# Attention scores from two fp32 parts in 64-row TensorE tiles in place of three bf16 parts in 32-column tiles, with the P.V products regrouped

## The reference, cut to what matters

```python
x = x + attention(layernorm(x))      # 16 heads of 8, softmax over all 512 keys
x = x + moe(layernorm(x))            # shared FFN 128-512-128, plus top 2 of 8 experts
# attention: q, k, v = x W.T + b ; softmax(q k.T / sqrt(8)) v ; out Wo.T + bo
```

## Time and profile before

| | us |
|---|---|
| median of 3 runs | 621.56 |
| span of the profiled execution | 600.2 |
| what lies around the span, by the median | 21.4 |
| PE busy | 585.2 (98%) |
| DVE busy | 497.1 (83%) |
| ACT busy | 452.8 (75%) |
| POOL busy | 280.1 (47%) |

### The profile page before, as it was taken

The page is one execution under the profiler, slowest core; times in us unless marked ns, Lnnn a source line. Parts: engine busy times, 40 slices in busy tenths (PEclk is TensorE's granted clock), DMA queues, the critical chain, the costliest instruction groups (busy, mean ns, idle before and its releaser), DMA issues.

```text
span 600.2 us, 21750 instructions
## 1 busy us (share of the span) xinstructions
PE 585.2 (98%) x8258; PEld 405.9 (68%) x8258; DVE 497.1 (83%) x1076; ACT 452.8 (75%) x967; POOL 280.1 (47%) x481
## 2 busy tenths in 40 slices
PE   6898999999999999999999999999999999999997
PEld 3443556555665655655655765656899999999966
DVE  8989999999999999999999999735577777777557
ACT  5887898888888888888888888985266555555551
POOL 7947430222542542542642642656745555555500
PEclk9999999999999999999999999999999999999999
DMA  6896333324434322322322311001422222222173
GB/s 177 224 303 208 110 80 93 102 79 121 126 91 128 90 57 61 85 57 64 82 57 66 82 56 47 21 20 49 93 56 67 70 70 70 71 70 70 42 294 136
DMA packets 43839, 57.66 MB, mean 96 GB/s; under 512 B 11130, under 2 KB 31482, under 8 KB 43754
## 3 DMA queue, kind: packets, MB, share of 16 engines
q1 hardware_dynamic: 39434, 47.59, 28.1%
q0 software_dynamic: 4320, 8.89, 4.6%
HBM read 35.76 MB, written 20.42 MB: 94 GB/s over the span
## 4 chain that ended last, share of the span: by engine, by line
PE 91%; ACT 3%; SPq 2%; DMA 1%; DVE 1%; issue 1%; POOL 0%; DVEq 0%; ACTq 0%
PE ps L1423 18%; PE ps L1451 18%; PE ps L1466 18%; PE ps L1677 11%; PE ps L1665 11%; PE ps L1624 4%; PE ps L1615 4%; PE ps L1405 2%; PE ps L1655 1%; PE ps L1486 1%; ACT xn L761 1%; PE ps L1411 1%; ACT probs L774 1%; PE ps L1497 1%; ACT probs L865 1%
## 5 line engine op out<-in xcount | busy, mean ns | idle before, releaser
L1002 DVE TENSOR_REDUCE mx<-ps 128x2 f32<-128x1024 f32 x256 | 306.2, 1212 | 20.2 <-PE ps L1423 12.2
L865 ACT ACTIVATE probs<-ps 128x512 f32<-128x512 f32 x512 | 296.8, 603 | 31.5 <-PE ps L1451 13.0
L1451 PE MATMUL ps<-q_op,k_op 128*32 128x512 bf16 x2048 | 205.0, 380 | 3.0 <-DMA q_op<-mxT 2.9
L1423 PE MATMUL ps<-k_op,q_op 96*32 96x512 bf16 x2048 | 161.0, 380 | 1.8 <-DVE mx L1002 1.3
L1466 PE MATMUL ps<-probs,v_op 128*32 128x256 f32 x2048 | 160.0, 378 | 0.0
L923 ACT ACTIVATE probs<-ps,b_cur 128x128 f32<-128x128 f32 x284 | 80.8, 368 | 59.4 <-PE ps L1665 58.6
L739 POOL DMA_INDIRECT results<-rest,row_id x71 | 71.6, 1009 | 66.5 <-DVE rest L1303 48.0
L1423 PEld LDWEIGHTS ps<-k_op,q_op 96*32 96x32 bf16 x2048 | 62.1, 97 | 52.9 <-DVE mx L1002 14.2
L1466 PEld LDWEIGHTS ps<-probs,v_op 128*32 128x32 f32 x2048 | 70.9, 109 | 38.7 <-ACT probs L865 0.2
L1451 PEld LDWEIGHTS ps<-q_op,k_op 128*32 128x32 bf16 x2048 | 64.5, 95 | 46.4 <-ACT probs L865 3.1
L630 POOL DMA_INDIRECT slots<-route_sb,slot_u x64 | 63.7, 995 | 58.0 <-ACT probs L865 49.7
(11 more groups left out here) (177 smaller groups left out, 543.0 us busy)
## 6 DMA issues: line engine op xcount, KB each, us to landing
q_op<-q_scr SPq DMA_DIRECT2D x96, 96.0 KB
k_op<-k_scr SPq DMA_DIRECT2D x96, 96.0 KB
w_sb<-in_W SPq DMA_DIRECT2D x18, 256.0 KB, 3.0
probs<-slots SPq DMA_DIRECT2D x71, 64.5 KB, 1.8
q_scr<-probs SPq DMA_DIRECT2D x8, 384.0 KB, 3.8
k_scr<-probs SPq DMA_DIRECT2D x8, 384.0 KB, 3.7
k_scr<-probs SPq DMA_DIRECT2D x8, 256.0 KB, 4.4
probs<-results SPq DMA_DIRECT2D x4, 512.0 KB, 4.8
```

Source lines behind the costliest of these rows:

```text
L865: nc.scalar.activation(probs[:, i, j, :], ps[:, BANK["key", b, hg, s], :], ACT.Exp, scale=float(D) ** -0.5).then_inc(s_exp, 1)
L1002: nc.vector.reduce_max(mx[:, slot % 2, 2 * p:2 * p + 2], ps[:, bank:bank + 2, :], AX.X).then_inc(s_max, 1)
L1423: last = nc.tensor.matmul(ps[c, BK_A + a % 4, :], q_op[hg][0:SH, j, P * i + c.start:P * i + c.stop], k_op[hg][0:SH, j, :], start=True, sto ...
L1451: last = nc.tensor.matmul(ps[c, bank, :], k_op[hg][:, j, P * i + c.start:P * i + c.stop], q_op[hg][:, j, :], start=True, stop=True)
```

## The change

- q and k are split in **two** parts of type float32r (read by TensorE in one pass) in place of three bf16 parts. ACT writes the first part (same instruction, other type), DVE the second (the same instruction as L993). L778 on ACT and L502 on POOL go away. For each head 4 products times 8 dimensions, 32 rows. `parts` has DEEP = 3 slots. A store is of 512 KB for q and 768 KB for k (before 384 KB and 640 KB). A group's operands come in 8 loads of 64 KB (before 6 of 96 KB).
- Two heads lie in one operand tensor, one at partitions 0 on, one at partitions 64 on. **A score tile is one matmul** of 128 stationary columns in a tile of 64 rows by 128 columns, and the tiles of two heads are issued one behind the other.
- The order on TensorE goes by two key tiles: keys s and s+1, the row pair, keys s+2 and s+3, the row pair, and then, once in four key tiles, a whole key tile's P.V in 32-column strips (both halves, 8 matmuls).
- `max_rows` transposes fp32 maxima (before bf16). The once-a-sequence work moves by a few steps, to stand behind P.V where it can.
- The FFN's working copies w1_cur and w2_cur and the last loads' targets lie in other SBUF buffers.

```diff
-PARTS = 3
+PARTS = 2
-SH = 96
+SH = KR + 1
-DEEP = 4
+DEEP = 3
-        N_LD = 6
+        N_LD, N_SH = 8, 2
-        PV_SLOTS = ((11, 12, 13, 15, 17, 19, 21, 23), (9, 11, 13, 15, 17, 19, 21, 23))
+        PV_AT = ((3, 3, 4, 5), (2, 3, 4, 5))
-        PROJECT_AT = (1, 2)
+        PROJECT_AT = (1, 3)
...
+        def head_of(s):
+            return s % 2 * JH + s % J // 2
...
-                nc.scalar.activation(parts[:, b % DEEP, w, 1, :], rest[:, b % 2, w, :], ACT.Copy).then_inc(s_mid, 1)
...
-                    nc.gpsimd.tensor_tensor(parts[:, b % DEEP, w, 2, :], rest[:, b % 2, w, :], parts[:, b % DEEP, w, 1, :],
-                                            ALU.subtract).then_inc(s_lo, 1)
...
             def row_scores(b, hg, p):
+                wait(pe, s_max, (b * HG + hg) * PAIRS + p - 1)
+                for half in range(2):
+                    at = ROW_HALF * half
+                    last = nc.tensor.matmul(ps[:, BK_A + 2 * (p % 2) + half, :], q_op[hg][at:at + rows, j, P * i:P * (i + 1)],
+                                            k_op[hg][at:at + rows, j, :], start=True, stop=True)
...
             def key_scores(b, hg, s):
-                for c in QUARTERS:
-                    last = nc.tensor.matmul(ps[c, bank, :], k_op[hg][:, j, P * i + c.start:P * i + c.stop], q_op[hg][:, j, :],
-                                            start=True, stop=True)
-                last.then_inc(s_sb, 1)
+                nc.tensor.matmul(ps[:, bank, :], k_op[hg][at:at + rows, j, P * i:P * (i + 1)], q_op[hg][at:at + rows, j, :],
+                                 start=True, stop=True).then_inc(s_sb, 1)
...
+            def products(b, hg, quad):
+                for i in range(NT):
+                    if PV_AT[(hg - 1) % 2][i] == NT + quad and b * HG + hg > 0:
+                        for half in range(2):
+                            pv((b * HG + hg - 1) // HG, (hg - 1) % HG, i, half)
+                for i in range(NT):
+                    if PV_AT[hg % 2][i] == quad:
+                        for half in range(2):
+                            pv(b, hg, i, half)
...
+                    for s in range(0, J * NT, 2):
+                        both = (s, s + 1)
+                        for n in both:
+                            key_scores(b, hg, n)
+                        for n in both:
+                            if (b, hg, n) in ROWS:
+                                pair = ROWS[b, hg, n]
+                                row_scores(pair // (HG * PAIRS), pair // PAIRS % HG, pair % PAIRS)
...
+                        if s % J == J - 2:
+                            products(b, hg, s // J)
```

More of the change, by code:

```diff
@@ L18 @@
-import struct
 import concourse.bass as bass
@@ L373, in load_group @@
                     sp.wait_ge(s_scr[b % DEEP], (b // DEEP + 1) * (16 * N_SCR))
[L374 to L377, removed]
+                for half in range(2):
+                    head, at = J * hg + JH * half, ROW_HALF * half
+                    for r in range(PARTS):
+                        for scr, op, first in ((q_scr, q_op, 0), (k_scr, k_op, D * r)):
+                            src = scr[b, :, :].rearrange("(x h) t -> x h t", h=H)[first:first + PR, head:head + JH, :]
+                            sp.dma_start(op[hg][at + PR * r:at + PR * (r + 1), :, :].bitcast(f32), src).then_inc(s_ld[hg], 16)
             def load_shift(b, hg):
@@ L382, in load_shift @@
                 sp.wait_ge(s_mxT, g + 1)
[L383 to L386, removed]
+                n = SHIFTS * JH * NT
+                for half in range(2):
+                    at = ROW_HALF * half + SH
+                    sp.dma_start(q_op[hg][at:at + SHIFTS, :, :].bitcast(f32).rearrange("o j (n t) -> o (j n) t", t=P),
+                                 mxT[n * half:n * (half + 1), hg % 2, :].bitcast(f32)).then_inc(s_sh[hg], 16)
             for b in range(B):
@@ L859, in exps @@
                         if g == 0 and i > 0:
[L860 to L863, removed]
+                            act.wait_ge(s_scr[i - 1], len(range(i - 1, B, DEEP)) * (16 * N_SCR))
+                        for s in range(i * J, (i + 1) * J):
+                            j = head_of(s)
                             act.wait_ge(s_sb, g * (J * NT) + s + 1)
@@ L986, in store_v, with second_part @@
                 nc.vector.tensor_copy(v_all[:, b, :, :], ps[:, v_bank(b), :].rearrange("p (n c) -> p n c", c=C)).then_inc(s_v, 1)
-            def take_rest(b, w):
+            def second_part(b, w):
                 bias, bank = ((bq_sb, q_bank(b)), (bk_sb, k_bank(b)))[w]
                 dve.wait_ge(s_hi, 2 * b + w + 1)
-                wait(dve, s_lo, 2 * (b - 2) + w + 1)
-                nc.vector.scalar_tensor_tensor(out=rest[:, b % 2, w, :], in0=ps[:, bank, :], scalar=bias[:, 0:1],
-                                               in1=parts[:, b % DEEP, w, 0, :], op0=ALU.add, op1=ALU.subtract).then_inc(s_rest, 1)
+                nc.vector.scalar_tensor_tensor(out=parts[:, b % DEEP, w, 1, :].bitcast(f32r), in0=ps[:, bank, :], scalar=bias[:, 0:1],
+                                               in1=parts[:, b % DEEP, w, 0, :], op0=ALU.add, op1=ALU.subtract).then_inc(s_lo, 1)
             def row_max(g, p, slot):
@@ L1171, in attend @@
                             last_max_out()
-                        if 3 <= p < 7 and hg == 2:
-                            out_norm(b, 0, p - 3)
-                        elif 3 <= p < 7 and hg == 0 and not first:
-                            out_norm(b - 1, 1, p - 3)
+                        if p >= 4 and hg == 2:
+                            out_norm(b, 0, p - 4)
+                        elif p >= 4 and hg == 0 and not first:
+                            out_norm(b - 1, 1, p - 4)
                         if not first:
@@ L1475, in max_rows @@
                 bank = wait_for_bank("mx", b, hg)
-                nc.tensor.matmul(ps[0:SHIFTS * J * NT, bank, 0:P], mx_parts[:, 0:SHIFTS * J * NT], id_bf[:, :],
+                nc.tensor.matmul(ps[0:SHIFTS * J * NT, bank, 0:P], mx_parts[:, :, :, :].rearrange("p h a n -> p (h a n)"), id_sb[:, :],
                                  start=True, stop=True).then_inc(s_mxTp, 1)
@@ L1600, in _ @@
             sequences(attend)
-            for k in range(2 * NT):
-                if PV_SLOTS[(HG - 1) % 2][k] >= J * NT:
-                    pv(B - 1, HG - 1, k // 2, k % 2)
+            for i in range(NT):
+                if PV_AT[(HG - 1) % 2][i] >= NT:
+                    for half in range(2):
+                        pv(B - 1, HG - 1, i, half)
             pe.wait_ge(s_wffn, 16 * N_WFFN)
```

142 lines of the change are left out of this document (51 added, 91 removed).

## The result

The changed kernel's median is **688.14 us** (681.19 to 697.18, 4 runs) against 621.4 for the kernel before (620.3 to 621.59, 4 runs). The ratio of 1.0973, 95% interval [1.0939, 1.1008], compares only the two faster runs (681.19 and 682.79 us, granted clock 0.939 and 0.937) with the kernel before, and leaves out the two at 0.916 and 0.912 (693.5 and 697.18 us); by the median of all four it would be 1.107. The direction was forecast. By that ratio the time is 682 us, at the range's upper end, and the median lies 6 us above it; the loss (61 us, or 67 by the median) is twice the 30 forecast. The profiled execution ran 682.79 us, its span is 681.0.

The account below looks back on a forecast made before the run. TensorE bound attention, DVE 6% behind. The new loop of 2.80 us per four key tiles made a sequence 49.2 against 44.8, 7.2 x 4.4 = +32; 600.2 + 32 + 21.4 = 653, stated as 652 us, range 608 to 682.

Parts of the forecast that it names:

- FFN and front, 0: FFN stays at 197.9 us, cost 0; the front's end could move by -3 to +5, taken as +0.
- late next in the front: In the front, the first group's exponentials, which write over `parts`, would wait until the last stores have landed; no size given.
- Direction: Whole kernel: slower with chance 0.71, faster 0.24, same 0.05.
- upper end of 682: Top of the whole-kernel range 608 to 682, reaching up to the case in which score tiles do not overlap.
- Two tiles side by side, 0.215 a pair: TensorE in attention: two 64-row score tiles run together in 0.215 us; without overlap 0.43.
- The rival without overlap: Attention: each score pair takes 0.43 us, 3.4 us more a sequence, +25, total 677; chance 0.13.
- Shape changes, 0.33: TensorE between scores and P.V: entering the wide shape 0.22, leaving about 0.1, together 0.33 us per four key tiles.
- The loop, 2.80: Attention: the fourth key tile waits for the first's exponential, with P.V in line: 2.80 us per four key tiles, before 2.60.
- The rival in which DVE sets the pace: Attention: shape changes and waited weight load cost almost nothing, loop 2.36, sequence 43.1, total 609 us; chance 0.22.
- The clock falls: Rival for TensorE in attention: at 1.2 GHz +1.3 us per four key tiles, +150 us; chance 0.02.
- 21.4 around the span: Whole kernel: median 621.56 lies 21.4 us above the profiled span of 600.2; added at the end of the sum.
- Looking at the profile after: Attention's expected signs: PEld wait about 0.5 us every fourth key tile, PE well under 100%, DVE near 85%, ACT near 80%.

Follow-up runs that it names:

- the pair on one chip: The kernel before and the changed kernel, both unchanged, run on the same chip: 624.31 us and 695.03 us.
- e3: Changed kernel with the split parts of q and k in buffers of their own, so the first group's exponentials don't wait for stores: 692.3 us.
- e7: Kernel before with only the order of P.V changed, one key tile's P.V behind each fourth key tile: 612.27 us, 1.0134 times before.
- e1: Changed kernel with the third of every four key tiles computed twice or three times into the same bank: 686.05 and 676.8 us.
- e2: Changed kernel with P.V in halves, one behind each two key tiles: 716.7 us (684.51 to 738.13), no ratio given.
- e1_fill2: Changed kernel with the third of every four key tiles computed three times into the same bank: 676.8 us, 1.0814 times before.
- e11: Changed kernel, unchanged, run again beside the kernel before on one chip: 695.03 us (686.17 to 706.81).
- e1_fill1: Changed kernel with the third of every four key tiles computed twice into the same bank: 686.05 us, 1.0931 times before.
- e8: Changed kernel with 64 active rows in key tiles and 62 in row scores, the further rows zeros: 663.06 us, 1.063 times before.

## Why the prediction was right, and where it failed

- **FFN and front, 0: right** (both shown by the pair on one chip). What was named as late next in the front came true (the exponentials waited for stores, 0.91 and 1.78) and cost nothing that e3 could show.
- **Direction and loop came true by their mechanism; that a time of 682 still meets the range is luck.** The loop gives 621 + 27 = 648 on this case's slower chips. The upper end of 682 stood for tiles that don't overlap, which did not happen; the clock brought the time there.
- **Two tiles side by side, 0.215 a pair: near.** Two key tiles together 0.51 against 0.49 for one, and the next tile follows 0.24 behind a pair. The rival without overlap (677, chance 0.13) is refuted. Part 3 of TensorE: Matmul & The Clock Gate in the Trainium skill would have made the pair an estimated 0.28; with two tiles of 64 rows the trace has 0.24, less than that.
- **Shape changes, 0.33: too small, inside its bounds of 0 to 0.5.** Last key tile to P.V is 0.66, of which 0.43 is streaming; P.V to the next key tile is 1.00, of which 0.86 is; then the row pair comes 0.34 after the key tile, 0.12 more than a stream. 0.23 + 0.14 + 0.12 = 0.49, but some of the 0.23 is the weight load behind the wait that I had counted apart with 0.11. The rule that a change of tiling mode drains TensorE (the Trainium skill, TensorEngine Tiling (Array Packing), Key Properties) agrees: e7, in one mode, goes from P.V to keys in 0.86.
- **The loop, 2.80: right in its parts, 2.91 measured.** By its parts: first to fourth key tile 1.25 (forecast 0.44 + 0.60 + 0.14 = 1.18), fourth to P.V 0.66 (0.54), P.V to the next quad 1.00 (1.08). e1 (more work is free) and e2 (P.V halved, 2.48) show that it is this ring. PEld waited 99.4 us in 200 waits, 0.50 each, as forecast. A sequence at 2.4 GHz is 49.8 (49.2). The rival in which DVE sets the pace is refuted: DVE idles 81.0 us for row scores.
- **The step that failed: "The clock falls", with 0.02 and as all or nothing (+150).** I took 1.00 in the rows of before for a reserve, and looked only for idle time. The clock fell in parts: 85 us or 13% of the span in the profiled run, worth about 34 of its 61 us, more than the loop's 27. Idle time is not what keeps it low: in the long stretch PE's records are busy 43.66 of 44.00 us, and in e1_fill2 the clock fell with no gap between records in the 21.6 us before. What the change alters on TensorE are, among other things, the active rows: 35 and 33 in place of 128 and 96. With 64 and 62 and nothing else changed, the time at 1.2 GHz went from 89 to 27 us and the ratio from 1.10 to 1.063, on one chip. That the rows matter is shown; that they are all of it is not, since 27 us are left, of which 7 lie in the front, where the kernel before has them too.
- **"21.4 around the span": wrong in kind, harmless in sum.** A run is 1.8 us longer than its span. The other 20 are, by its span, another chip: the profile of before fits one on which it runs in 602 to 606 us. On the chip that runs it in 621 to 627 a sequence of before is 46.0, so the loop cost 27 there, not 32.
- **Looking at the profile after**: ACT's share was to be near 80% and is 68% (35.06 of 51.40), and PE's well under 100% and is 93%. An exponential's record is no shorter (607 ns against 603), but now they come back to back, 0.49 apart, so their records overlap and the same 512 fill 263.2 us in place of 296.8. Busy shares forecast worse than starts.

Open: what starts the long stretch. In all ten profiles of kernels with the changed scores the clock falls between 50.8 and 54.3 us, around the first key tile and its gap of 2.1 us. It then stays low for 10 to 17 us in the four with 64 rows, and for 51 to 92 in four of those with 35; in the other two (e11 and e1_fill1) for 17, and again for 48 from 139.5 on. Open too: why it ends; why halves lowered the clock so much with 35 rows (0.81 to 0.90) and little or not at all with 64 (0.957 to 0.979); whether the wider column tile (128 in place of 32), the other type or the change of shapes has a part. Active rows beyond 64 can't be had in these tiles, and a P.V in another type than fp32 wasn't tried.

## What to carry to other kernels

When instructions are regrouped, walk the ring between two in-order engines (tile, exponential, buffer free, next tile) and count all that stands in it, P.V and shape changes too; here it set 2.91 us where DVE's work was 2.26 and TensorE's 1.72, both by the prediction's sum. A change that makes TensorE's work thinner can cost clock even where its records leave no gap, so a granted clock of 1.00 before promises nothing for operands of fewer rows; price a partial fall, not only a full one. And compare the spans of two kernels only on one chip.

## What the runs showed of the hardware

- The granted clock of TensorE stayed at 1.2 GHz for 51 us, and from 60 to 104 us of it with records busy 43.66 of 44.00. The mean clock rose from 0.935 to 0.979 when tiles of 35 and 33 active rows got 64 and 62, at equal times (e11 and e8, one chip). The Trainium skill (TensorE: Matmul & The Clock Gate, Part 1, HAM oscillation) ties the lower clock to TensorE standing idle. The start of the long stretch, behind a gap of 2.1 us, may agree; the falls in e1_fill2 do not, since the one at 179.7 us came with records busy 21.60 of 21.60 us before it, and the measurement decides.
- Two fp32r tiles of 64 rows by 128 columns start 4 ns apart and run side by side (0.51 us for both, 0.49 for one, 512 columns each). A tile behind such a pair starts 0.24 us after it, and a record of its 128-column weight load is 0.18 us.
- P.V to scores: 1.00 us with a change of tile shape, 0.86 without.
- Two chips of one kind ran the same program in 604 and 624 us, at a granted clock of 0.994 to 1.0 on both.
